# Decoder bodies written out instead of looped, and a new instruction order that asks for the first norm later in a body

## The reference

```python
for i in range(4):                                   # L = 4 layers, D = 256, 16 heads of 16, F = 1024
    xn = layer_norm(x, ln1_w[i], ln1_b[i])           # "the first norm"
    qkv = xn @ Wi.T + bi                             # 256 -> 768
    scores = q @ k.T / 4 + alibi + causal mask       # per head, 256 x 256
    x = x + softmax(scores) @ v @ Wo.T + bo
    xn = layer_norm(x, ln2_w[i], ln2_b[i])           # "the second norm"
    x = x + gelu(xn @ W1.T + b1) @ W2.T + b2         # 256 -> 1024 -> 256
```

## Time and profile before

| | us |
|---|---|
| median of 3 runs (3950.48 to 3954.08) | 3953.2 |
| the profiled execution's own time | 3950.34 |
| its span, first to last instruction | 3948.5 |
| PE busy in the span (89%) | 3497.6 |
| DVE busy (60%) | 2361.2 |
| ACT busy (48%) | 1892.8 |
| POOL busy (36%) | 1415.3 |

### The profile page before, as it was taken

How to read it: one execution, slowest core, us unless ns; L and a number is a source line. 1 busy time by engine, 2 the same in 40 slices (tenths; PEclk the granted TensorE clock), 3 DMA queues, 4 the chain that set the end, 5 groups by cost and what they waited for, 6 DMA issues and landing times. The chain is left out here.

```text
span 3948.5 us, 98572 instructions
## 1 busy us (share of the span) xinstructions
PE 3497.6 (89%) x37088; PEld 2401.6 (61%) x37088; DVE 2361.2 (60%) x4859; ACT 1892.8 (48%) x2713; POOL 1415.3 (36%) x1324
## 2 busy tenths in 40 slices
PE   5899999999999999999955667679999999999998
PEld 3566666666666676666633444446666666666666
DVE  5777777777767777777436676444444434434356
ACT  4666676666766667766623333332222322223222
POOL 1243233332333323333323222134444444444443
PEclk8999999999999999999977778789999999999999
DMA  3100111001110011100011111020000000000000
GB/s 110 45 24 29 45 33 45 27 26 45 33 45 27 26 45 33 45 27 26 18 49 38 44 37 33 23 113 11 11 22 0 22 0 22 20 2 11 0 12 32
DMA packets 103895, 124.22 MB, mean 31 GB/s; under 512 B 17664, under 2 KB 94208, under 8 KB 101120
## 3 DMA queue, kind: packets, MB, share of 16 engines
q1 hardware_dynamic: 103520, 118.78, 9.1%
HBM read 50.13 MB, written 8.39 MB: 15 GB/s over the span
## 5 line engine op out<-in xcount | busy, mean ns | idle before, releaser
L2088 POOL TENSOR_TENSOR e_hT<-e_h,e_hT 128x512 f16<-128x512 f32 x512 | 591.1, 1156 | 775.4 <-DVE e_hT L2054 775.4
L75 PE MATMUL bank<-e_half,e_hT 128*128 128x256 f16 x6144 | 713.7, 273 | 2.6 <-POOL e_hT L2088 2.5
L991 DVE TENSOR_REDUCE mx<-maxima_pair 128x4 f16<-128x1024 f32 (+1 forms) x384 | 470.2, 1224 | 376.8 <-PE maxima_pair L482 374.9
L75 PEld LDWEIGHTS bank<-e_half,e_hT 128*128 128x128 f16 x6144 | 601.8, 98 | 127.2 <-issue 3.3
L2054 DVE CAST e_hT<-e_h 128x512 f16<-128x512 f32 x512 | 301.2, 591 | 448.0 <-ACT e_h L2012 447.8
L75 PE MATMUL bank<-xT,w_half 128*128 128x512 f16 x2304 | 535.4, 383 | 29.4 <-ACT mrow L770 18.3
L1091 POOL TENSOR_TENSOR QK<-qk,QK 128x512 f16<-128x512 f32 x128 | 148.1, 1157 | 1026.3 <-ACT QK L721 985.9
L789 ACT ACTIVATE PR<-scores_pair 128x1024 f32<-128x1024 f32 x384 | 393.0, 1024 | 177.5 <-PE scores_pair L499 97.2
L2012 ACT ACTIVATE e_h<-scores_pair,e_b 128x512 f32<-128x512 f32 x256 | 175.9, 687 | 495.1 <-PE scores_pair L75 449.0
L1098 POOL TENSOR_TENSOR hT<-h,hT 128x512 f16<-128x512 f32 x256 | 291.9, 1168 | 296.8 <-ACT hT L776 296.8
L2012 ACT ACTIVATE e_h<-maxima_pair,e_b 128x512 f32<-128x512 f32 x256 | 175.7, 687 | 456.8 <-PE maxima_pair L75 445.1
(11 more groups left out here) (162 smaller groups left out, 5676.1 us busy)
## 6 DMA issues: line engine op xcount, KB each, us to landing
QS<-QK SPq DMA_DIRECT2D x240, 128.0 KB, 2.1
KS<-QK SPq DMA_DIRECT2D x192, 128.0 KB, 2.1
e_raw<-in_expert_weights SPq DMA_DIRECT2D x16, 1024.0 KB, 5.1
w_raw<-in_weights SPq DMA_DIRECT2D x48, 256.0 KB, 3.1
c_x<-in_x SPq DMA_DIRECT2D x8, 512.0 KB, 4.2
xT_halves<-c_xT SPq DMA_DIRECT2D x16, 256.0 KB, 2.6
out<-e_z SPq DMA_DIRECT2D x8, 512.0 KB, 2.9
x<-in_x SPq DMA_DIRECT2D x1, 3584.0 KB, 15.3
```

Source lines behind the costliest of these rows:

```text
L75: last = pe.matmul(out, stat(a, k), mov(b, k), start=(k == 0 and n == 0), stop=(k == tiles - 1 and n == 2))
L991: dve.tensor_reduce(out, src, AX.X, ALU.max, negate=True).then_inc(mx_in.sem, 1)
L2088: pool.tensor_tensor(low, h32[:, m % 2, :], hT[odd][0][:, m, :], ALU.subtract)\
```

## The change

Two things change, both in the decoder. First, the two loops over bodies become Python loops, so every body stands in the program with constant semaphore values, on all five engines. Second, the five `body` functions and the list `tiles_of` get a new order. The computation is the same, instruction for instruction of arithmetic. The core of the diff (line numbers of the new kernel are some lines lower):

```diff
-        with eng.Fori(0, L - 1) as l:
-            with eng.Fori(2, NG - 2) as g:
+        for l in range(L - 1):
+            for g in range(2, NG - 1):
                 run(STEADY, l * NG + g, g, 0, None)
-            run(STEADY, l * NG + NG - 2, NG - 2, 0, None)
             run(STEADY, l * NG + NG - 1, NG - 1, 1, l + 1)
...
-        out = f(("V", 0, 1)) + b(("OS", 0)) + a(("T1", 0)) + b(("OS", 1, 2)) + a(("T1", 1)) + b(("OS", 3))
+        out = f(("V", 0)) + b(("OS", 0, 1, 2, 3)) + f(("V", 1)) + b(("OT", 0)) + a(("T1", 0)) + b(("OT", 1))
...
-        out += t(("Y", 3)) + a(("MT", 0)) + b(("H", 0, 1, 2, 3, 4, 5, 6, 7)) + a(("MT", 1))
+        out += b(("H", 0, 1, 2, 3)) + a(("MT", 0)) + b(("H", 4, 5, 6, 7)) + a(("MT", 1))
...
@@ SP
             if ahead:
-                heads_low(n + 1, 1)
                 heads_high(n + 1, 1)
...
                 maximum(n + 1, 0)
+                heads_low(n + 1, 1)
                 maximum(n + 1, 1)
...
@@ ACT
             if front:
+                exps(n, 0, 0)
                 values(kind, n, 0)
-                exps(n, 0, 0)
+                exps(n, 0, 1)
                 values(kind, n, 1)
...
@@ DVE
             if swap == 3:
                 weights(l, "f2")
             if ahead:
+                maxima(n + 1, 1, 0)
                 maxima(n + 1, 1, 1)
...
@@ POOL
+            if front:
+                values(n, 0)
+                values(n, 1)
             if ahead:
                 query_key_low(n + 1, 0)
                 query_key_low(n + 1, 1)
...
```

More of the change, by code:

```diff
@@ L316, in all_bodies @@
         n = (L - 1) * NG
-        with eng.Fori(2, NG - 2) as g:
+        for g in range(2, NG - 1):
             run(STEADY, n + g, g, 0, None)
-        run(STEADY, n + NG - 2, NG - 2, 0, None)
         run(LAST, n + NG - 1, NG - 1, 0, None)
@@ L572, in body @@
                 values(kind, n, 0)
+            if back:
+                turn_outputs(kind, n, 0)
+                turn_outputs(kind, n, 1)
+            if front:
+                key_scores(n, 0, 1)
+            if back:
+                turn_outputs(kind, n, 2)
+                turn_outputs(kind, n, 3)
+            if front:
+                row_scores(n, 2, 1)
                 values(kind, n, 1)
             if back:
-                turn_outputs(kind, n, 0)
+                pe.wait_ge(on_in.sem, on_in.after(n - 1))
+                turn(kind, n, "OT", 0, OT_ps, On)
             if ahead:
@@ L579, in body @@
             if front:
-                row_scores(n, 2, 1)
-                key_scores(n, 0, 1)
+                key_scores(n, 0, 2)
+                row_scores(n, 2, 2)
             if back:
[L583 to L591, removed]
+                turn(kind, n, "OT", 1, OT_ps, On)
             if tail:
                 shrunk(kind, n, 0)
-            if back:
-                pe.wait_ge(on_in.sem, on_in.after(n - 1))
-                turn(kind, n, "OT", 0, OT_ps, On)
             if front:
@@ L599, in body @@
                 key_scores(n, 1, 0)
-            if back:
-                turn(kind, n, "OT", 1, OT_ps, On)
             if ahead:
[L603 to L611, removed]
+                turn(kind, n, "T1", 1, T1_ps, z[0])
             if back:
@@ L616, in body @@
             if front:
-                row_scores(n, 3, 2)
-                key_scores(n, 1, 2)
+                turn_maxima(kind, n, n, 2)
+                attend(n, 0)
+                key_scores(n, 1, 1)
+                row_scores(n, 3, 1)
             if back:
                 attended(kind, n, 1)
+            if ahead:
+                if swap == 1:
+                    part_ready("qkv", l)
+                queries_keys(kind, n, 0)
+                queries_keys(kind, n, 1)
+            if front:
+                key_scores(n, 1, 2)
+                row_scores(n, 3, 2)
             if ahead:
@@ L636, in body @@
             if front:
-                key_scores(n, 2, 1)
-                attend(n, 1)
+                key_scores(n, 2, 2)
+            if back:
+                turn(kind, n, "T2", 1, T2_ps, z[1])
+            if ahead:
+                queries_keys(kind, n, 3)
+            if front:
+                key_scores(n, 3, 0)
             if ahead:
                 row_scores(n + 1, 0, 1)
[L641 to L649, removed]
             if tail:
@@ L659, in body @@
             if ahead:
-                row_scores(n + 1, 1, 1)
-                turn_maxima(kind, n, n + 1, 0)
+                row_scores(n + 1, 1, 0)
             if back:
@@ L667, in body @@
             if ahead:
-                row_scores(n + 1, 1, 2)
+                row_scores(n + 1, 1, 1)
             if back:
@@ L671, in body @@
                 hidden(kind, n, 3)
+            if ahead:
+                row_scores(n + 1, 1, 2)
+                turn_maxima(kind, n, n + 1, 0)
+            if back:
                 hidden(kind, n, 4)
@@ L861, in body @@
                 exps(n, 2, 2)
+            if back:
+                norm2(kind, n, 0)
+                norm2(kind, n, 1)
+            if front:
                 exps(n, 3, 0)
@@ L870, in body @@
                 exps(n, 3, 1)
-            if back:
-                norm2(kind, n, 1)
-            if front:
+                out_rows(n, 2)
                 exps(n, 3, 2)
@@ L1015, in body @@
             if back:
[L1016 to L1020, removed]
+                outputs_low(kind, n, 0)
             if front:
@@ L1025, in body @@
             if ahead:
-                low(0, n + 1, 1, xh1, xf1, xl1)
+                low(0, n + 1, 0, xh1, xf1, xl1)
+            if back:
+                outputs_low(kind, n, 1)
             if tail:
@@ L1030, in body @@
                 maxima(n, 3, 0)
[L1031 to L1036, removed]
+            if ahead:
+                low(0, n + 1, 1, xh1, xf1, xl1)
             if back:
```

110 lines of the change are left out of this document (54 added, 56 removed).

## The result

The changed kernel took 3819.26 us in the median of 4 runs (3816.29 to 3822.59), the kernel before 3952.86 (3950.48 to 3954.08, 4 runs): a ratio of 0.9663, 95% interval 0.9646 to 0.968. The profiled execution has a span of 3814.5 us, 134.0 less than before. The forecast was 3842, that is 111 less. The direction, the range and the mechanism of an ordinary body held, and the saving was a fifth larger, most of the excess from bodies that the forecast had counted at nothing.

The account below looks back on a forecast made before the run. PE was taken to bound the 29 steady bodies: 1591.5 work + 45 ordinary waits + 20 weights + 5 clock = 1661.5 us instead of 1772.1, 110.6 less, giving 3842 us; 8-in-10 range 3796 to 3912.

Parts of the forecast that it names:

- PE bounds the body, and each body has either a jump or a norm wait: Steady bodies: PE loses 137.9 us in waits, 53.6 at 14 jumps back and 42.0 in 15 waits for z.
- a fall of the clock follows each of these waits: Steady bodies: the clock falls right behind a jump or norm wait; low stretches cost 42.7 us in all.
- The loops, 28 us: Jumps back in the steady stretch: each costs 2.0 us more than the norm wait it hides, 14 x 2.0 = 28 us.
- my walk through the body: Order of an ordinary new body: norm ends at 3.6, PE waits 1.55 us, other close meetings counted at nothing.
- The norm's start and length: First norm on DVE: norm_var starts at -4.0, z ends at 3.6 instead of 6.7, as POOL's add_row leave its run.
- the stricter reading: First norm, DVE getting nothing in POOL's gaps: ends at about 4.4, 0.8 later, sum 23 us higher.
- What PE meets then: PE in an ordinary body: 0.25 us wait at the third turn_outputs, 1.3 at the fourth; 29 x 1.55 = 45 us.
- The bodies with weights and the clock: Swap bodies in the steady stretch: conversions cost 3 x 6.8 = 20 us of waits; 5 of 42.7 us of low clock kept.
- The six filling and draining bodies, at nothing: Before and behind the steady stretch: change counted at nothing, 10 us either way staying in the range.
- The wait only moves: Rival: norm needed later but ready as much later, only the loops' 28 us come; 3925 us, chance 12%.
- Slower: Rival: norm's length does not shrink, fourth turn_outputs waits 7.5 us a body; 4060 us, decides from about 10 us; chance 9%.
- The clock stays low: Rival: something still makes the clock fall once a body, 38 us of the gain lost; 3880 us, chance 14%.

Follow-up runs that it names:

- experiment 1: The kernel before with its loops written out and the old order on all engines; 3908.5 us, ratio 0.9894.
- experiment 2: The changed kernel with the two loops kept, new order on all engines; 3856.3 us, ratio 0.9769.
- experiment 3: The changed kernel with POOL's add_row put back among the hidden_low and its last query_key_low ahead of them; 3989.9 us, ratio 1.0105.
- experiment 4: The kernel before, written out, with only POOL's order taken from the change; 3812.8 us, ratio 0.9655.
- Experiment 5: The kernel of experiment 4 with ACT's first exps of a body ahead of its first values; 3776.8 us, ratio 0.9561.

## Why the prediction was right, point by point

*PE bounds the body, and each body has either a jump or a norm wait.* Held: experiment 1 turns the 15 waits for `z` into 29 and removes the 14 others. That a fall of the clock follows each of these waits did not hold: body 15 waits 2.8 us for `z` and stays at 1.00 over its whole length:

```profile
948.92 0.66 PE L447 MATMUL bank<-ident,z 128*128 128x128 f32 x4 [2.82 <-DVE z L142]
```

*The loops, 28 us.* Mis-sized: 41. By the lists of waits, the 14 jumps less the waits for `z` that take their place are 18.0 us (53.6 less 35.6), small waits for ACT that stood behind the jumps and are gone 5.9, and `mrow` 18.3. I had expected the wait for `mrow` gone for another reason, the new place of its tile. Either is enough: experiment 1 loses it in the old order, and experiment 2 has none although its table load is late. The 28 us is no term of the sum, and my walk through the body had no wait for `mrow`, so the sum didn't suffer.

*The norm's start and length.* Start at -4.0 and length 7.6 were forecast, -4.0 and 7.55 measured. POOL's run as the cause is shown from both sides: put back, it makes the norm 11.45 us and the kernel slower than before (experiment 3, with one instruction of `values` in that length); alone, it shortens the norm from 12.97 to 9.24 us and brings as much as the whole new order (experiments 1 and 4). The norm ended at 3.5, against 3.6 in the walk and 4.4 in the stricter reading, because DVE uses the gaps between POOL's instructions (945.42, 946.78 and 948.07 to 948.6). That stricter reading went beyond what it named. The Trainium skill (SBUF — State Buffer, Who interferes with whom) states a lock that is held for one instruction, and that leaves the gaps open. The trace agrees: the four instructions of 1.1 us end within 0.05 us of a `hidden_low` (945.38 and 945.36 the first), and those in the gaps are not held.

*What PE meets then.* 1.3 at the fourth `turn_outputs` and 0.25 at the third were forecast, 1.07 and none measured: 14 us less in 29 bodies (45 to 30.9).

*The bodies with weights and the clock.* Mis-sized: 25 us forecast (20 and 5). By the starts of the bodies, the six with conversions of swap 1 and 3 exceed 55.92 by 33 us together. Swap 3 came as forecast (1.5, 0.6 and 2.3 us of waits against 4.8), swap 1 not: 3.5 us of wait instead of 2, and the clock fell behind it, to 0.57 over four microseconds:

```profile
899.50:903.50 4.00, 3.38 (x37) 2.89 (x38) 2.39 (x3) 1.27 (x2) 0.00 (x0) 0.57 0.00 0
```

Behind the 1.07 it did not fall: the ordinary bodies take 55.91 to 55.93 us, but for one of 55.72, all at 1.00. The two errors of the steady stretch, 15 us too much in the ordinary bodies and 8 too little in those with weights, partly cancel.

*The six filling and draining bodies, at nothing.* This is the step that failed, a term put at nothing: the drain is 16.6 us shorter, most of what the forecast missed. In the drain PE waited 8.7 us for POOL's `hT` before and waits 2.7 now. The drain took 134.0 us in experiment 1, 128.8 in experiment 4 and 124.7 in experiment 3: POOL's order alone gives 5.2 of it, written-out bodies 1.4, and the remaining 10 comes from the other engines' orders. I had set a bound of 10 us either way; which engine's order gives the rest was not tried.

*The rivals.* "The wait only moves" is true of the place and not of the size: the wait stands at `On` now, with 30.9 us instead of the 95.6 of `z` and the jumps. "Slower" was a fair warning: 3990 us is what the same order costs when POOL's run stays long, with a length of 11.45, beyond the 10 from which it was to decide. "The clock stays low" did not come: 0.99 over the stretch.

*What the order was for.* The change in a few words says that the first norm is needed later. No gain from that part is shown. Experiment 4, which needs it as early as before, is level with the changed kernel. Experiment 5 adds one piece of the new order, ACT's exp first, and is 40 us faster than the changed kernel (0.9561 against 0.9663), so the rest of the new order on PE, DVE, ACT and SP costs time on balance; which piece costs it, the reader's place or another, was not tried. With POOL's run long, the new order is 81 us slower than the old one (experiments 1 and 3). Some 30 of these, by the estimate there, are the instruction of `values`. For the others the rows show this: the fourth `turn_outputs` asks at 4.3 us of the body, and what it needs is ready 1.9 us behind `z`, where the old order needed only `z`, at 4.0.

## What to carry to other kernels

When an engine's small instructions are several times slower in one place than in another, look at what its neighbour does at that time before moving the reader: moving POOL's work was worth 96 us (experiments 1 and 4), and the new orders of the other four engines together nothing on top. A wait can be taken away only down to the next thing that the late engine owes, so walk its queue on from the result that was waited for. And price the filling and draining bodies too: they wait more than the steady ones (PE is idle 34.7 of the drain's 118.9 us in the changed kernel, and 54.9 of the 1654.5 of the steady bodies).

## What was not expected of the hardware

- The load of the gelu table on ACT starts early where the semaphore value behind it is a constant, and late where it is in a register: 490.07 right behind an exp, against 990.11 behind a wait of 1.09 us for PE in the looped kernel, whose one body outside the loops loads early too. In the old order it cost 18.3 us of PE's time, in the new one none.
- A jump back to a loop's start left PE idle for 3.1 to 4.4 us or not at all: all fourteen did in the kernel before, seven of fourteen in the profiled execution of the second experiment.
- Where the norm's small instructions and POOL's `hidden_low` or `add_row` meet, DVE pays nearly alone: `hidden_low` has a mean of 1157 ns after and 1168 before, with more of the norm beside it, while DVE's small instructions go from 0.17 to 0.65 or 1.1 us.
- A wait of PE of 2.8 to 2.9 us is followed by a fall of the granted clock in some bodies (0.55 behind body 14's) and not in others (body 15, 1.00 throughout). What decides is left open.
